# Attention: the two blocks of narrow matmuls that close a unit are put side by side

## The reference

```python
q = (query @ Wq + bq).reshape(B, Nq, H, D).transpose(0, 2, 1, 3)
k = (key_value @ Wk + bk).reshape(B, Nkv, H, D).transpose(0, 2, 1, 3)
v = (key_value @ Wv + bv).reshape(B, Nkv, H, D).transpose(0, 2, 1, 3)
attn = jnp.clip(jnp.einsum('bhqd,bhkd->bhqk', q, k) * scale, -CLAMP, CLAMP)
attn = jax.nn.softmax(attn, axis=-1)
x = jnp.einsum('bhqk,bhkd->bqhd', attn, v).reshape(B, Nq, Cq)
return x @ Wo + bo                      # then x + tanh(g) * ..., and the feed-forward
```

## Time and profile before

| | |
|---|---|
| time, median of 3 runs | 3110.64 us |
| the profiled execution's own time | 3112.01 us |
| its span | 3110.2 us |
| TensorE busy | 2996.1 us, 96% |
| VectorE / ScalarE / GpSimd busy | 2119.5 / 1709.5 / 1837.2 us |
| mean granted TensorE clock | 0.98 of full |

### The profile page before, as it was taken

The page is one execution under the profiler, slowest core; times in us unless marked ns, Lnnn a source line. Parts: engine busy times, 40 slices in busy tenths (PEclk is TensorE's granted clock), DMA queues, the critical chain, the costliest instruction groups (busy, mean ns, idle before and its releaser), DMA issues. The chain is left out here.

```text
span 3110.2 us, 51282 instructions
## 1 busy us (share of the span) xinstructions
PE 2996.1 (96%) x15462; PEld 1807.1 (58%) x15462; DVE 2119.5 (68%) x3020; ACT 1709.5 (55%) x3096; POOL 1837.2 (59%) x887
## 2 busy tenths in 40 slices
PE   8999979999999999999999999999969799999999
PEld 6888854444444444444444444444426577777777
DVE  5555557676676767667676666767647787777775
ACT  3222227776766767767776767767732344444443
POOL 4655548888888888888888888888844000000000
PEclk9999989999999999999999999999989799999999
DMA  6667742222212222221221222122159200000000
GB/s 203 226 220 237 226 173 62 54 49 61 60 42 61 61 49 53 61 59 43 61 61 46 56 61 56 46 61 60 24 148 292 109 28 28 18 25 26 21 21 28
DMA packets 139855, 254.72 MB, mean 82 GB/s; under 512 B 16946, under 2 KB 57970, under 8 KB 132596
## 3 DMA queue, kind: packets, MB, share of 16 engines
q1 hardware_dynamic: 139764, 253.60, 28.9%
HBM read 162.32 MB, written 91.23 MB: 82 GB/s over the span
## 5 line engine op out<-in xcount | busy, mean ns | idle before, releaser
L836 DVE TENSOR_REDUCE at_half_max<-ps 128x1 f32<-128x1024 f32 x1024 | 1208.7, 1220 | 542.0 <-PE ps L654 534.9
L583 POOL TENSOR_TENSOR at_gp_sum<-at_gp_sum,at_probT 128x1024 f32<-128x1024 f32 x512 | 1218.2, 2379 | 42.3
L778 ACT ACTIVATE at_probT<-ps 128x512 f32<-128x512 f32 x2048 | 1060.0, 603 | 226.5 <-PE ps L673 226.5
L654 PE MATMUL ps<-k_stack,q_stack 96*128 96x512 f32 x2048 | 701.6, 424 | 15.8 <-issue 12.1
L673 PE MATMUL ps<-q_stack,k_stack 98*128 98x512 f32 x2048 | 659.8, 403 | 1.6 <-ACT at_probT L778 1.3
L654 PEld LDWEIGHTS ps<-k_stack,q_stack 96*128 96x128 f32 x2048 | 345.0, 191 | 397.0 <-issue 222.5
L712 PE MATMUL ps<-at_probT,v_head 128*32 128x512 f32 x4096 | 492.5, 598 | 0.9 <-ACT at_probT L778 0.9
L673 PEld LDWEIGHTS ps<-q_stack,k_stack 98*128 98x128 f32 x2048 | 385.9, 189 | 171.2 <-ACT at_probT L778 99.3
L578 POOL TENSOR_TENSOR at_gp_sum<-at_probT 128x1024 f32<-128x1024 f32 x128 | 305.2, 2384 | 298.1 <-ACT at_probT L778 298.1
L1383 POOL TENSOR_TENSOR x_keep<-x_keep,b_half 128x2048 f32<-128x2048 f32 x8 | 37.5, 4682 | 550.4 <-DVE x_keep L1406 550.4
L1436 DVE SCALAR_TENSOR_TENSOR ff_acc<-ps,s_t,ff_acc 128x512 f32<-128x512 f32 x384 | 288.0, 750 | 20.3 <-PE ps L1312 0.4
(11 more groups left out here) (172 smaller groups left out, 3638.8 us busy)
## 6 DMA issues: line engine op xcount, KB each, us to landing
k_stack<-kT_hi SPq DMA_DIRECT2D x128, 256.0 KB, 5.0
kT_hi<-pi_out_hi SPq DMA_DIRECT2D x16, 1024.0 KB, 4.4
kT_lo<-pi_out_lo SPq DMA_DIRECT2D x16, 1024.0 KB, 6.7
v_heads<-pi_v_out SPq DMA_DIRECT2D x16, 1024.0 KB, 10.4
q_stack<-qT_hi SPq DMA_DIRECT2D x128, 128.0 KB, 3.4
k_stack<-kT_lo SPq DMA_DIRECT2D x64, 256.0 KB, 4.3
v_head<-v_heads SPq DMA_DIRECT2D x64, 256.0 KB, 5.1
pi_c_in<-in_ctx_dram SPq DMA_DIRECT2D x16, 768.0 KB, 9.9
```

The lines of the kernel that those rows point to most:

```text
L583: pool.tensor_tensor(gp_sum[lane % 2][:, :, :], gp_sum[lane % 2][:, :, :], pairs[:, 2 * i + 2:2 * i + 4, :], ALU.add).then_inc(gp_added, 1)
L654: mm = pe.matmul(ps[:, n, :], q_stack[buf][0:PARTS, rows], k_stack[buf][0:PARTS, BANK * n:BANK * (n + 1)], start=True, stop=True)
L778: act.activation(probT[lane % 2][:, kv, :], src, ACT.Exp).then_inc(exp_done, 1)
L836: dve.tensor_reduce(dst, src, AX_X, ALU.max).then_inc(max_done, 1)
```

## The change

```diff
-    TURN, KEYS, PV, SUMS, FOLD = 5, 6, (9, 10), 11, 12
+    TURN, KEYS, PV, SUMS, FOLD = 5, 6, (9, 10), 12, 12
```

## The result

The changed kernel takes 3102.94 us (median of 10 runs, 3101.59 to 3104.31), the kernel before 3110.18 in the same comparison (10 runs); the ratio is 0.9978, 95% interval 0.9968 to 0.9988. 3103.0 was forecast from 3110.64. The profiled execution has a span of 3101.6 us; the attention in it is 7.98 us shorter than in that of the kernel before (from the first S to the end of the last copy, 1848.64 for 1856.62).

What follows compares the result with a forecast made beforehand. TensorE alone was taken to bound the attention stage, with VectorE late next once blocks join. From 3110.64 us, -1.3 over the units and -6.3 at the loop jumps gave 3103.0 us, range 3098 to 3108.

Steps and rivals of the forecast that it cites:

- TensorE alone, 0.34 us a unit: Joining fold and last sums removes one narrow block's entry and exit on TensorE, 0.34 us at 125 places, 42.5 us.
- What is late next: VectorE's two maxima (2.36 us) outlast phase 3's wide pairs (1.88), so scores wait twice; net -0.01 us a unit, -1.3 us.
- the refill paid twice: After each of two TensorE waits for VectorE, S23 of phase 3 and S01 of phase 0, the pair takes 0.10 us more.
- The jump: At 19 loop jumps VectorE, now 0.8 us earlier, swallows its 0.35 us issue gap; TensorE gains 0.33 each, -6.3 us.
- TensorE's own jump: TensorE's loop jump, ahead of S01 of phase 0, hides behind the VectorE wait; rival: it shows, 3109 to 3112, 10%.
- The sum: Whole kernel: -1.3 us per-unit effect and -6.3 us at the loop jumps, together -7.6 us, 3103.0 us.
- Rival 4: TensorE's clock falls to 1.2 GHz in phases 3 and 0; in one unit of ten some 75 us, 3185; 2%.

## Why the prediction was right

- *TensorE alone, 0.34 us a unit*: the block takes what V takes, and with VectorE out of the way 0.29 come through. Right; the 0.05 that are missing are ScalarE's, which the prediction hadn't set against this case.
- *What is late next*: VectorE, at the two places named, with the refill paid twice. Each start was right within 0.02 us. -0.01 us a unit was forecast; the measured half unit has -0.004 on average, -0.02 in the one shown. The other half, which was to stay as it was away from the jumps, has -0.019 there, 2 us in all. Neither can be told from nothing: two executions of one kernel (VectorE's loop written out) had median units of 14.286 and 14.307, which makes 2.6 us over 125 units.
- *The jump*, 19 x 0.33 = 6.3: measured 19 x 0.33 in the trace, and 6.5 to 7.5 when the gaps were taken away by themselves. This term is nearly all of the gain. Right.
- *TensorE's own jump*: "waits for VectorE anyway" holds, but narrowly; it is 0.3 us long, and 0.03 of it shows. It was sound to keep it as a rival.
- *The sum* of -7.6 met -7.2. The profiled spans differ by 8.5: 9.2 in the steady units (the 19 jumps 6.3, the rest 2.9), 0.8 ahead of the attention, less 1.2 of the fallen clock at its end and 0.3 behind. The ten executions of each kernel spread over 2.7 and 4.0 us, so the mechanism and the size of about 7 us are confirmed, and that the sum came within half a microsecond is luck.
- *Rival 4*, the clock: it did fall, once and briefly, at the attention's end and not in the wide phases. The prediction had taken the full clock in those 26 us as a sign that idle time there is harmless; this is the one reading that did not hold. With waits of 1.1 us in place of the 0.1 here, in the kernel with the block joined in phase 3, it fell in the middle of the attention too, behind 3 of 19 jumps. So rival 4 names a thing that happens; in the changed kernel the waits were short.

## What to carry to other kernels

Joining two blocks of one kind saves an entry and an exit, but the stretch that it empties runs at the pace of the next engine; before the gain is counted, put the starts of every engine in that stretch in a row, each wait with its refill. Count all instructions of each engine there, the copies in between too: the one I left out turned a forecast of 3098 into 3145. And a gain may come from a place that the change isn't about, here from slack that covers the loop's gap on another engine.

## What the runs showed of the hardware

- A wait of 0.07 us on TensorE (K to S 0.54 instead of 0.47) cost 0.17: the pair behind it took 0.57 instead of 0.47. The weight load (PEld) waits with it and is no longer hidden: it starts at 1505.70 together with its matmul, where that of the pair at 1504.69, which doesn't wait, starts at 1504.46.
- TensorE began 0.055 us after the end of the VectorE instruction that it waited for (median of 123 units at each of the two places).
- The jump back of a loop costs VectorE 0.35 us and TensorE 0.3 (K to S 0.75 for 0.50 beside it), the latter in full only in the kernel with short maxima, where the stretch ahead has nothing but wide matmuls and no wait behind the jump covers it. With a narrow block in phase 3, ahead of the jump, K to S stayed 0.47.
- A satisfied wait in the middle of a block of narrow matmuls costs nothing: second half 0.89 after the first, of 1.86.
- The clock can fall for 3.4 us behind a stretch where TensorE is busy for 4.40 of 5 us; with the same stretch (4.41 of 5 us) it stayed full in another execution of nearly the same program. It fell so behind 3 of 19 waits of 1.1 us in the kernel with the block joined in phase 3.
